# Between two transformer layers: paired powers, denominators on VectorE, and loads behind the first expert tiles

## The chip, the cores and the metric

The kernel runs on one core of a Trainium2 chip. The metric is the device time of one execution in microseconds (us). Matrix products run on TensorE (PE), elementwise work on VectorE (DVE), ScalarE (ACT) and GpSimd (POOL); SyncE (SP) issues most of the DMAs. The engines run side by side and wait for one another by semaphores only.

## The reference, cut to what matters

Thirty-two sequences of 128 rows of width 128 pass two layers, each with a residual attention and a residual feed-forward block. Layer 0's feed-forward block is a routed one with eight experts, and its routing is what the change touches:

```python
x = x + xattn0(layernorm(x), ctx, ctx)
n = layernorm(x)                          # eps 1e-5
num = einsum('bsd,ed->bse', n, waff)
aff = num / (norm(n) * norm(waff) + 1e-9) # the denominators
tcr = one_hot(argmax(softmax(aff)), 8)    # the chosen expert
ranks = argsort(argsort(-aff, axis=1), axis=1)
dispatch = tcr * (ranks < cap)            # cap from mean(aff)
x = x + sum_e(gelu((n*dispatch_e) @ W1_e + b1_e) @ W2_e + b2_e)
x = x + xattn1(layernorm(x), ctx, mask)   # 16 heads of 64, a null key and value
x = x + bitlinear_ffn(layernorm(x))       # ternary weights, 8-bit activations
```

## The kernel before, in words

The program is written by hand for each engine: an engine runs its instructions in the order in which its function issues them, and every dependency across engines, and most within one, is a `wait_ge` on a semaphore.

**Layer 0's attention and routing** (`attention_routing_block`) loops over the 32 sequences b. Beside the attention, each finished row block r is normalised and routed. VectorE takes mean and variance (`residual_stats`, into `stats2`); GpSimd adds epsilon and takes the power -0.5 (`route_norm`, L235); the normalised rows `xn2` are written by GpSimd, from r = 27 on by VectorE (`route_scale`, L743); TensorE transposes them (`route_transpose`) and multiplies with the router's weights (`affinity`, L367); VectorE copies the eight scores out (`num_copy`). The 32 blocks are routed in five groups (`GROUPS`), the last two of four blocks each. For a group, GpSimd works out the denominators in five instructions (`denominators`, L247); VectorE chooses an expert for each row in ten (`choose`: reciprocal, affinity and its maximum, a one-hot choice `tcrb`, and `seen`, the running count per expert); TensorE turns the choices into places in a sorted list (`places`, L369), in the last group behind a product `countp` that gives the counts of all rows; VectorE reads the places off (`locate`). Then GpSimd sends each block's 128 rows to their places in DRAM by an indirect DMA (`scatter`, L270). The rows of block r can go once their group is located and `xn2` is there. After the loop GpSimd does block 30's norm, scatter 24, block 31's norm, the last denominators, and scatters 25 to 31, in that order.

**Between the layers.** When the last variance is there (`l0["done"]`), SyncE issues 17 loads (`sync_weights`, L1426: layer 1's value weights, norm scales and biases, masks, null key and value, two context blocks and three feed-forward weights); the constants' loads all count on one semaphore `w_in`. TensorE fills its gaps with sums over the experts' output weights (`sums_part`, L1000), in eight parts of eight products; then come products for layer 1 (`Setup.tensor`, L1641, L1644, L1649), which wait for `w_in` (15 loads) and VectorE's list.

**The expert block** (`expert_block`) turns the counts into a list of at most 39 tiles (VectorE, L1137 to L1149; `tau` is the tile's place, `eid` its expert; ready as `from_dve` LIST). SyncE waits for the list and all scatters, then loads tiles of 128 rows, six slots ahead (`sync_part`, L947: six loads, the store of `Cc`, then one load for each slot that comes free). TensorE transposes tile i (L1019), multiplies it up (L1027) and down (L1039); the order on TensorE is up(i+1), transpose(i+2), down(i). GpSimd copies each tile's weights, ScalarE does the Gelu, VectorE adds the bias and, from tile to tile, also ranks rows and prepares layer 1: the null key's shift at tile 4, masks and context statistics at 8, weight magnitudes at 10.

**Layer 1** (`attention_ffn_block`) then gathers the rows back and loops over the 32 sequences.

Of the kernel before, what the change touches and what calls it, by code (L numbers as in the profile page):

```python
# [5 lines left out]
ALU = mybir.AluOpType  # L6
# [38 lines left out]
def routing_state(nc, space, ctx):  # L45


    B, E, G = 32, 8, 8

    def sb(name, shape, dt=F32):  # L50
        return space.enter_context(nc.sbuf_tensor("r_" + name, shape, dt))

    def sem(name):
        return ctx.enter_context(nc.semaphore("r_" + name))

    t = dict(
        waffT=sb("waffT", [P, E]), wsq=sb("wsq", [P, E]), wsum=sb("wsum", [P, E]), wn=sb("wn", [P, E]),
        ones=sb("ones_f", [P, P]), ones_b=sb("ones_b", [P, P], BF16), before_t=sb("before_t", [P, P], BF16),
        weight=sb("weight", [P, E]), region=sb("region", [P, E]),
        vpe=sb("vpe", [P, 2]), rs2=sb("rs2", [P, B]), spread=sb("spread", [P, G]), xnorm=sb("xnorm", [P, G]),  # L60
        xnT=sb("xnT", [P, 2, P]), num=sb("num", [P, B, E]), den=sb("den", [P, 2, G, E]), aff=sb("aff", [P, B, E]),
        mval=sb("mval", [P, B]), tmp=sb("tmp", [P, G, E]), score=sb("score", [P, G, E]), smax=sb("smax", [P, G]),
        tcr=sb("tcr", [P, B, E]), tcrb=sb("tcrb", [P, B, E], BF16), gsum=sb("gsum", [P, E]),
        seen=sb("seen", [P, 6, E], BF16),
        place=sb("place", [P, G, E]), posf=sb("posf", [P, B]), pos_s=sb("pos_s", [P, B], I32),
        zeros=sb("zeros", [P, 704]))
    s = {n: sem(n) for n in ("w_in", "set", "wsq", "wsum_done", "wsum", "wn", "rs2", "den", "xn2", "xnt", "xnT",
                             "num_done", "num", "choice", "place_done", "place", "z_out", "scat")}
    return t, s


def attention_routing_block(nc, ctx, space, consts, x, ctxT, w, wr, x_res, xn2, stats2, psum, dram):
# [19 lines left out]
    LATE = 28  # L92

# [48 lines left out]
    countp = xp[:, S + 16:S + 16 + E]  # L142
# [51 lines left out]
    def pool_part(g, after_setup, before_loop):  # L194
# [51 lines left out]

        def denominators(q):  # L247
            a, z = GROUPS[q]
            cols, n = slice(a, z), z - a
            spread, xnorm, den = rt["spread"][:, 0:n], rt["xnorm"][:, 0:n], rt["den"][:, q % 2, 0:n, :]  # L250
            den_seq, first = rsem["den"], 5 * q
            g.wait_ge(rsem["rs2"], 2 * z)
            nc.gpsimd.tensor_scalar(spread, stats2[:, cols, 1], float(D), None, ALU.mult).then_inc(den_seq, 1)
            g.wait_ge(den_seq, first + 1)
            nc.gpsimd.tensor_tensor(xnorm, spread, half[:, 0:n], ALU.pow).then_inc(den_seq, 1)
            g.wait_ge(den_seq, first + 2)
            nc.gpsimd.tensor_tensor(spread, xnorm, rt["rs2"][:, cols], ALU.mult).then_inc(den_seq, 1)
# [29 lines left out]
        for b in range(B):  # L287
# [4 lines left out]
            if b >= 2:  # L292
                route_norm(b - 2)
# [11 lines left out]
        route_norm(B - 2)  # L305
        scatter(scattered)
        scattered += 1
        route_norm(B - 1)
        denominators(NG - 1)
# [3 lines left out]
    def tensor_part(pe, expert_sums_part):  # L313
# [55 lines left out]
        def places(q):  # L369
# [12 lines left out]
            if q == NG - 1:  # L382
                pe.wait_ge(rsem["choice"], 10 * q + 10)
                nc.tensor.matmul(countp, rt["ones_b"][:], rt["seen"][:, q + 1, :], start=True, stop=True)
            nc.tensor.matmul(at_, rt["before_t"][:], rows[:, a:z, :].rearrange("p b e -> p (b e)"),
                             start=True, stop=False, skip_group_check=True)
            for j in range(n - 1):
# [3 lines left out]
                             start=False, stop=True, skip_group_check=True).then_inc(rsem["place_done"], 1)  # L391

# [208 lines left out]
    def vector_part(dve):  # L601
# [27 lines left out]

        def choose_reciprocal(q):  # L630
            a, z = GROUPS[q]
            n, seq = z - a, rsem["choice"]
            dve.wait_ge(rsem["den"], 5 * q + 5)
# [41 lines left out]
        def choose(q):  # L675
            choose_reciprocal(q)
# [60 lines left out]
        def residual_stats(b, s):  # L737
# [3 lines left out]
            nc.vector.bn_aggr(stats2[:, b, :], bn2[:, s, :]).then_inc(x1_stats, 1)  # L741

        def route_scale(r):  # L743
            dve.wait_ge(rsem["rs2"], 2 * r + 2)
            dve.wait_ge(rsem["xn2"], r)
            nc.vector.tensor_scalar(xn2[:, r, :], x_res[:, r, :], stats2[:, r, 0:1], rt["rs2"][:, r:r + 1],
# [14 lines left out]
        for b in range(B):  # L761
# [35 lines left out]
            elif b >= 1:  # L797
# [11 lines left out]
        route_scale(B - 1)  # L809
        num_copy(B - 1)  # L810
# [4 lines left out]
                done=(x1_stats, 3 * B), half_done=(x1_stats, 3 * (B // 2)), exp_done=(exp_ready, 4 * B), pv_free=(oev_ready, B), actp_free=(rsem["xnT"], B), countp=countp, route=route)  # L815


def make_consts(nc, ctx):
    def sb(name, shape, dt=F32):
# [4 lines left out]
             mask=sb("head_rows", [P, 16]), mask4=sb("group_rows", [P, 4]), minus_half=sb("minus_half", [P, 32]), half=sb("half", [P, 32]))  # L824

    def pool_part(g):
# [4 lines left out]
        nc.gpsimd.memset(c["half"][:], 0.5)  # L831
        nc.gpsimd.memset(c["mask"][:], 1.0).then_inc(ready, 1)
# [34 lines left out]
def expert_block(nc, ctx, space, consts, w, psum, dram, route, l0, pos_g):  # L867
# [79 lines left out]
    def sync_part(sp):  # L947
# [7 lines left out]
        for i in range(XT):  # L955
            load(i)
        sp.wait_ge(from_dve, CDS)
# [168 lines left out]
    def vector_part(dve, layer1_setup):  # L1126
# [9 lines left out]

        seq.then(nc.vector.tensor_scalar(ne[:], l0["countp"], float(P - 1), 1.0 / P, ALU.add, ALU.mult))  # L1137
# [142 lines left out]
def attention_ffn_block(nc, ctx, consts, w, wff, early, x_res, psum, before, gathered, out):  # L1280
# [68 lines left out]
    w_in, p_set, setup_done = sem("w_in"), sem("p_set"), sem("setup_done")  # L1349
    sa_done = sem("sa_done")  # L1350
# [27 lines left out]
    N_W = 15 * 16  # L1378
# [47 lines left out]
    def sync_weights(sp):  # L1426
        sp.dma_start(Wv[:], w["Wv"]).then_inc(w_in, 16)
        for t, n in ((s1, "ln1_s"), (b1, "ln1_b"), (sc_, "lnc_s"), (bc, "lnc_b")):
            sp.dma_start(t[:], w[n].rearrange("(d a) -> d a", a=1)).then_inc(w_in, 16)
        sp.dma_start(so_row[:], w["lno_s"].partition_broadcast(P)).then_inc(w_in, 16)  # L1430
        sp.dma_start(bo_row[:], w["lno_b"].partition_broadcast(P)).then_inc(w_in, 16)
        sp.dma_start(mask8[:], w["maskT"]).then_inc(w_in, 16)
        sp.dma_start(mrow8[:], w["mask"].partition_broadcast(P)).then_inc(w_in, 16)
        sp.dma_start(nk_row[:], w["nk"].partition_broadcast(P)).then_inc(w_in, 16)
        sp.dma_start(nv_row[:], w["nv"].partition_broadcast(P)).then_inc(w_in, 16)
        sp.dma_start(nv_col[:], w["nv2"]).then_inc(w_in, 16)
# [190 lines left out]
    class Setup:  # L1627
# [52 lines left out]
        def masks(self, dve, part):  # L1680
            bs = slice(8 * part, 8 * part + 8)
# [373 lines left out]
    def scalar_part(act):  # L2055
        act.wait_ge(w_in, N_W)
# [345 lines left out]
    return dict(sync_early=sync_early, sync_weights=sync_weights, sync=sync_part, pool_setup=pool_setup, gpsimd=pool_part, tensor=tensor_part,  # L2402
# [4 lines left out]
def two_layers(nc, d, out):  # L2407
# [5 lines left out]
    with ExitStack() as ctx:  # L2413
# [31 lines left out]
        def _(sp):  # L2445
# [5 lines left out]
            ex["sync"](sp)  # L2451
# [74 lines left out]
```

## Time and profile before

| | |
|---|---|
| median of 3 runs | 812.02 us (808.96 to 813.08) |
| the profiled execution's own time | 812.02 us |
| its span, first to last instruction | 810.3 us |
| TensorE busy in the span | 763.3 us, 94% |
| VectorE, GpSimd, ScalarE busy | 673.7, 477.8, 440.4 us |
| mean granted TensorE clock | 0.983 of 2.4 GHz |

Busy time is the union of an engine's instructions over the span, and overlapping engines don't add up. Layer 0 ends at some 206 us, the expert tiles run from 222 to 307 us, and layer 1 fills the rest. Which of the engines sets the time of a stretch is read from the chain of waits: it goes back from the last instruction of a window to whatever released it.

### The profile page before, as it was taken

Reading aid. Unit: us, or ns where it says so; the run is one execution under the profiler, and the core shown is the slowest. Engines: PE = TensorE matmul, PEld = TensorE weight load, DVE = VectorE, ACT = ScalarE, POOL = GpSimd, SP = SyncE. Lnnn points to the kernel's source line nnn. Section 1 sums busy time; section 2 is a strip of 40 time slices with the busy share of each in tenths; the row PEclk is TensorE's granted clock in tenths of the full one; section 3 lists DMA queues with packets and bytes.
Section 4 is the critical chain, followed back from the end, with each engine's and each line's share of the span. In section 5 each row is a group of like instructions: output and inputs, shape, how many; then the busy total and the mean of one; then the engine's idle time right before and its main releaser. Section 6 shows DMA issues by size and latency. Waiting matters only on the chain.

```text
span 810.3 us, 28859 instructions
## 1 busy us (share of the span) xinstructions
PE 763.3 (94%) x10843; PEld 642.5 (79%) x10873; DVE 673.7 (83%) x1775; ACT 440.4 (54%) x1078; POOL 477.8 (59%) x912
## 2 busy tenths in 40 slices
PE   8999999998799997999999999999999999999973
PEld 6777777776699996788888888878888888888861
DVE  6888889877757764689998999989989999999876
ACT  4666666656066663455564554555545655556542
POOL 7767678887857763345564655645645546554334
PEclk9999999999999998999999999999999999999996
DMA  8986220000422211121141141241231212212130
GB/s 240 372 350 253 110 87 15 17 21 28 141 70 67 60 46 34 38 64 46 42 78 54 46 87 45 53 80 46 62 71 45 81 52 62 70 45 77 39 44 14
DMA packets 68253, 65.81 MB, mean 81 GB/s; under 512 B 23714, under 2 KB 49042, under 8 KB 68114
## 3 DMA queue, kind: packets, MB, share of 16 engines
q1 hardware_dynamic: 53250, 39.71, 18.8%
q10 hardware_dynamic: 12816, 20.06, 6.7%
q0 software_dynamic: 2048, 4.20, 1.8%
q8 instruction: 86, 1.41, 0.7%
q14 instruction: 53, 0.43, 0.2%
HBM read 35.89 MB, written 24.37 MB: 74 GB/s over the span
## 4 chain that ended last, share of the span: by engine, by line
PE 37%; DVE 29%; DMA 18%; issue 6%; SPq 6%; POOL 2%; ACT 1%; DVEq 1%; another core or an unknown queue 0%; POOLq 0%; ACTq 0%
DMA a_r_all<-a_r_rows 10%; DMA a_r_rows<-a_rT 7%; SPq L1464 6%; DVE a_mxf L2222 5%; PE psum L1039 4%; PE psum L432 4%; PE psum L421 4%; PE psum L1027 4%; PE psum L414 3%; DVE a_rT L2238 3%; DVE f_h L2311 3%; DVE a_oT L2247 3%; DVE f_hm L2317 2%; DVE f_xt L2296 2%; PE psum L403 2%
## 5 line engine op out<-in xcount | busy, mean ns | idle before, releaser
L2079 ACT ACTIVATE a_pT<-psum 128x512 f32<-128x512 f32 x128 | 69.5, 595 | 50.9 <-PE psum L1888 35.0
L1571 POOL TENSOR_TENSOR f_hd<-f_hmc,a_wmean 128x1 f32<-128x1 f32 x32 | 6.7, 210 | 133.1 <-DVE f_hr L2322 131.9
L720 DVE TENSOR_REDUCE l_mx<-psum 128x4 bf16<-128x512 f32 x128 | 81.8, 680 | 3.5 <-PE psum L403 1.9
L2222 DVE TENSOR_REDUCE a_mxf<-psum 128x8 f32<-128x1024 f32 x64 | 77.5, 1210 | 4.6 <-PE psum L1857 4.6
L1800 PEld LDWEIGHTS psum<-a_cTm,a_Wk 128*128 128x128 f32 x512 | 64.1, 191 | 19.8 <-issue 19.8
L1788 PEld LDWEIGHTS psum<-a_xT,a_Wq 128*128 128x128 f32 x512 | 65.0, 193 | 15.4 <-issue 14.0
L552 ACT ACTIVATE l_pT<-psum 128x512 f32<-128x512 f32 x128 | 70.5, 597 | 8.1 <-PE psum L421 7.8
L1565 POOL TENSOR_SCALAR f_hq<-f_ht 128x512 bf16<-128x512 f32 x31 | 60.3, 1946 | 20.0 <-ACT f_ht L2122 19.9
L1867 PE MATMUL psum<-a_qT,a_kT 64*128 64x128 f32 x1024 | 71.9, 281 | 0.0
L1788 PE MATMUL psum<-a_xT,a_Wq 128*128 128x128 f32 x512 | 70.3, 281 | 0.6 <-ACT a_xT L2062 0.6
L1835 PE MATMUL psum<-a_Wv,a_cTm 128*128 128x512 f32 x128 | 70.1, 633 | 0.2
L1800 PE MATMUL psum<-a_cTm,a_Wk 128*128 128x128 f32 x512 | 70.2, 281 | 0.0
L2122 ACT ACTIVATE f_ht<-f_h,f_big_m,f_hr 128x512 f32<-128x512 f32 x32 | 26.0, 814 | 81.1 <-DVE f_hr L2322 79.0
L1867 PEld LDWEIGHTS psum<-a_qT,a_kT 64*128 64x128 f32 x1024 | 63.0, 190 | 0.0
L1901 PE MATMUL psum<-a_pT,a_v 128*32 128x128 f32 x2048 | 62.8, 274 | 0.1
L1815 PE MATMUL psum<-a_Wo,a_oT 128*128 128x128 f32 x512 | 62.6, 276 | 0.0
L1901 PEld LDWEIGHTS psum<-a_pT,a_v 128*32 128x32 f32 x2048 | 53.9, 110 | 8.4 <-DVE a_oT L2247 4.3
L1815 PEld LDWEIGHTS psum<-a_Wo,a_oT 128*128 128x128 f32 x512 | 59.7, 192 | 0.2 <-issue 0.2
L421 PEld LDWEIGHTS psum<-negI,l_mx 128*128 128x128 bf16 x512 | 35.3, 100 | 25.0 <-DVE l_mx L720 22.7
L2109 ACT COPY a_v<-psum 128x512 f32<-128x512 f32 x64 | 37.5, 585 | 23.1 <-PE psum L1835 23.1
L2247 DVE TENSOR_TENSOR a_oT<-psum,a_r_all 128x512 f32<-128x512 f32 x64 | 42.1, 679 | 9.5 <-issue 5.9
L1100 ACT ACTIVATE e_hT<-psum,e_w1t 128x128 f32<-128x128 f32 x156 | 44.5, 368 | 6.5 <-issue 5.8
(313 smaller groups left out, 2067.9 us busy)
## 6 DMA issues: line engine op xcount, KB each, us to landing
sorted_x<-r_zeros ACTq DMA_DIRECT2D x12, 1408.0 KB, 7.1
a_r_all<-a_r_rows SPq DMA_DIRECT2D x124, 128.0 KB
e_xt<-sorted_x SPq DMA_DIRECT2D x39, 64.0 KB, 1.8
sorted_y<-e_yt ACTq DMA_DIRECT2D x39, 64.0 KB, 1.6
e_w<-in_E_W1b SPq DMA_DIRECT2D x1, 2064.0 KB
a_cin<-in_ctx SPq DMA_DIRECT2D x32, 64.0 KB, 2.6
out<-f_x SPq DMA_DIRECT2D x32, 64.0 KB, 2.2
x_res<-in_x SPq DMA_DIRECT2D x1, 512.0 KB, 5.5
```

The source lines that it names most:

```text
L421: last = nc.tensor.matmul(tp[k][:, j * S:(j + 1) * S], mx[:, b % 2, h:h + 1].to_broadcast([P, P]), negI[:], start=False, stop=(j == Q4 - 1 ...
L552: nc.scalar.activation(pT[:, k, :], tp[k], ACT.Exp, scale=SCALE).then_inc(exp_ready, 1)
L720: nc.vector.tensor_reduce(mx[:, s, Q4 * k:Q4 * k + Q4], maxp[k % 2].rearrange("p (h t) -> p h t", h=Q4), AX_X, ALU.max).then_inc(mx_ready, 1)
L1788: last = nc.tensor.matmul(bank[:, i * S:(i + 1) * S], Wq[:, 4 * half + i, :], xT[:, b % 2, :], start=True, stop=True)
L1800: last = nc.tensor.matmul(bank[:, i * S:(i + 1) * S], Wk[:, 4 * half + i, :], cTm[:, b % 2, :], start=True, stop=True)
L1815: last = nc.tensor.matmul(pa[:, 0:D], oT[:, p, :], Wo[:, p, :], start=(p == 0), stop=(p == NP - 1))
L1835: nc.tensor.matmul(bank, cTm[:, b % 2, :], Wv[:, 512 * half:512 * half + 512], start=True, stop=True).then_inc(v_done, 1)
L1867: last = nc.tensor.matmul(tp[e][:, i * S:(i + 1) * S], kT[r, b % 2, p, :], qT[r, b % 2, p, :], start=(half == 0 and i == 0), stop=(half == ...
L1901: last = nc.tensor.matmul(op[half][32 * j:32 * j + 32, i * S:(i + 1) * S], v[:, b % 2, 8 * half + 4 * e + i, part], pT[:, 2 * half + e, i ...
L2079: nc.scalar.activation(pT[:, 2 * half + e, :], tp[e], ACT.Exp, scale=SCALE).then_inc(exp_ready, 1)
L2222: nc.vector.tensor_reduce(mxf[:, 8 * half:8 * half + 8].rearrange("p (e h) -> p e h", e=2), psum[:, 0:2, :].rearrange("p e (h t) -> p e h ...
L2247: nc.vector.tensor_tensor(oT[:, 4 * half:4 * half + 4, :].rearrange("p n q -> p (n q)"), op[half], r_all[:, half, :], ALU.mult).then_inc(o ...
```

## The change

Five edits, all around the end of layer 0. (1) For blocks 28 to 31 VectorE writes both bases, variance + 1e-5 and 128 x variance, into `spans`, and GpSimd takes both roots in one power on two columns (`paired_roots`) in the place of `route_norm`. (2) The last group's denominators move from GpSimd to VectorE: three instructions ahead of the reciprocal, and both go ahead of block 31's `num_copy`. (3) The count product goes behind the places in the last group, into another bank, and VectorE waits for it where it starts the list. (4) On TensorE `affinity(31)` goes ahead of the third part of the expert sums, and all but three parts go behind the last places. (5) Of `sync_weights` five loads stay; twelve go behind the first six tile loads (`sync_late`), with semaphores of their own that their readers wait for. The constant `pair` costs six one-column memsets at the start.

```diff
+    PAIRED = GROUPS[-1][0]
-    countp = xp[:, S + 16:S + 16 + E]
+    countp = yp[:, 3 * S:3 * S + E]
...
+        def paired_roots(r):
+            i = r - PAIRED
+            g.wait_ge(rsem["spans"], i + 1)
+            nc.gpsimd.tensor_tensor(rt["roots"][:, i, :], rt["spans"][:, i, :], consts["pair"][:, 0, :], ALU.pow).then_inc(rsem["roots"], 1)
...
-            if b >= 2:
+            if b - 2 >= PAIRED:
+                paired_roots(b - 2)
+            elif b >= 2:
                 route_norm(b - 2)
...
-        route_norm(B - 2)
+        paired_roots(B - 2)
         scatter(scattered)
         scattered += 1
-        route_norm(B - 1)
-        denominators(NG - 1)
+        paired_roots(B - 1)
         for r in range(scattered, B):
             scatter(r)
...
-            if q == NG - 1:
-                pe.wait_ge(rsem["choice"], 10 * q + 10)
-                nc.tensor.matmul(countp, rt["ones_b"][:], rt["seen"][:, q + 1, :], start=True, stop=True)
             nc.tensor.matmul(at_, rt["before_t"][:], ...
...
                              start=False, stop=True, skip_group_check=True).then_inc(rsem["place_done"], 1)
+            if q == NG - 1:
+                pe.wait_ge(rsem["choice"], 10 * q + 10)
+                nc.tensor.matmul(countp, rt["ones_b"][:], rt["seen"][:, q + 1, :], start=True, stop=True).then_inc(rsem["place_done"], 1)
...
         route_transpose(B - 1)
+        affinity(B - 1)
         expert_sums_part(2, 3)
-        affinity(B - 1)
-        expert_sums_part(3, 5)
         places(NG - 1)
-        expert_sums_part(5, E)
+        expert_sums_part(3, E)
...
+        def last_denominators():
+            n, seq, den = B - PAIRED, rsem["last_den"], rt["den"][:, (NG - 1) % 2, 0:B - PAIRED, :]
+            dve.wait_ge(rsem["roots"], n)
+            nc.vector.tensor_tensor(rt["last_spread"][:], rt["roots"][:, :, 0], rt["roots"][:, :, 1], ALU.mult).then_inc(seq, 1)
+            dve.wait_ge(seq, 1)
+            nc.vector.tensor_tensor(den, rt["last_spread"][:].unsqueeze(2).broadcast_to([P, n, E]),
+                                    rt["wn"][:].unsqueeze(1).broadcast_to([P, n, E]), ALU.mult).then_inc(seq, 1)
+            dve.wait_ge(seq, 2)
+            nc.vector.tensor_scalar(den, den, 1e-9, None, ALU.add).then_inc(seq, 1)
...
             nc.vector.bn_aggr(stats2[:, b, :], bn2[:, s, :]).then_inc(x1_stats, 1)
+            if b >= PAIRED:
+                dve.wait_ge(x1_stats, 3 * b + 3)
+                nc.vector.scalar_tensor_tensor(out=rt["spans"][:, b - PAIRED, :], in0=consts["pair"][:, 1, :], scalar=stats2[:, b, 1:2],
+                                               in1=consts["pair"][:, 2, :], op0=ALU.mult, op1=ALU.add).then_inc(rsem["spans"], 1)
...
         route_scale(B - 1)
+        last_denominators()
+        choose_reciprocal(NG - 1)
         num_copy(B - 1)
         choose(NG - 1)
         locate(NG - 1)
...
+        for i, (first, second) in enumerate(((-0.5, 0.5), (1.0, float(P)), (EPS_BLOCK, 0.0))):
+            nc.gpsimd.memset(c["pair"][:, i, 0:1], first)
+            nc.gpsimd.memset(c["pair"][:, i, 1:2], second)
...
         for i in range(XT):
             load(i)
+        after_first_tiles()
         sp.wait_ge(from_dve, CDS)
...
+        dve.wait_ge(rsem["place_done"], l0["groups"] + 1)
         seq.then(nc.vector.tensor_scalar(ne[:], l0["countp"], float(P - 1), 1.0 / P, ALU.add, ALU.mult))
...
-    N_W = 15 * 16
+    N_W, N_LATE = 8 * 16, 5 * 16
...
     def sync_weights(sp):
         sp.dma_start(Wv[:], w["Wv"]).then_inc(w_in, 16)
-        for t, n in ((s1, "ln1_s"), (b1, "ln1_b"), (sc_, "lnc_s"), (bc, "lnc_b")):
+        for t, n in ((sc_, "lnc_s"), (bc, "lnc_b")):
             sp.dma_start(t[:], w[n].rearrange("(d a) -> d a", a=1)).then_inc(w_in, 16)
...
+        sp.dma_start(nv_col[:], w["nv2"]).then_inc(w_in, 16)
         sp.dma_start(mask8[:], w["maskT"]).then_inc(w_in, 16)
...
+    def sync_late(sp):
+        sp.dma_start(nk_row[:], w["nk"].partition_broadcast(P)).then_inc(null_in, 16)
+        sp.dma_start(nv_row[:], w["nv"].partition_broadcast(P)).then_inc(null_in, 16)
         for b in range(2):
             sp.dma_start(cin[:, b, :], w["ctx"][b]).then_inc(cin_ld[b], 16)
+        sp.dma_start(mrow8[:], w["mask"].partition_broadcast(P)).then_inc(late_in, 16)
+        for t, n in ((s1, "ln1_s"), (b1, "ln1_b")):
+            sp.dma_start(t[:], w[n].rearrange("(d a) -> d a", a=1)).then_inc(late_in, 16)
+        sp.dma_start(so_row[:], w["lno_s"].partition_broadcast(P)).then_inc(late_in, 16)
+        sp.dma_start(bo_row[:], w["lno_b"].partition_broadcast(P)).then_inc(late_in, 16)
         sp.dma_start(wf[:, 0, :], wff["gateT"]).then_inc(f_in, 16)
...
         def null_shift(self, dve, which):
             if which == 0:
                 dve.wait_ge(lift_seq, 4)
+                dve.wait_ge(null_in, 2 * 16)
...
         def masks(self, dve, part):
+            if part == 0:
+                dve.wait_ge(late_in, N_LATE)
```

## Rows read from the trace of the kernel before

**Rows 1.** The page: the span.

```profile
span 810.3 us, 28859 instructions
```

**Rows 2.** Chain of waits, 185 to 232 us: start us, us, what.

```profile
208.76 0.20 DVE r_aff L642
...
216.47 2.33 DMA sorted_x<-xy,r_pos_s
...
219.85 1.74 DMA e_xt<-sorted_x
```

**Rows 3.** Timeline, 196 to 236 us: start, us, engine, operation, idle before.

```profile
204.89 0.25 POOL L238 TENSOR_SCALAR r_vpe<-stats 128x1 f32<-128x1 f32 x1
...
205.22 0.57 POOL L240 TENSOR_TENSOR r_rs<-r_vpe,minus_half 128x1 f32<-128x1 f32 x1
...
207.29 0.29 PE L367 MATMUL psum<-r_waffT,r_xnT 128*128 128x8 f32 x2
...
208.73 1.10 POOL L270 DMA_INDIRECT sorted_x<-xy,r_pos_s  x1 [0.39 <-issue]
...
209.88 0.19 DVE L663 TENSOR_TENSOR r_tcrb<-r_score,r_smax 128x32 bf16<-128x32 f32 x1
...
210.76 0.17 PE L384 MATMUL psum<-r_seen,r_ones_b 128*128 128x8 bf16 x1 [1.30 <-DVE r_seen L673]
...
210.91 2.92 PE L1000 MATMUL psum<-e_w,e_gb 128*128 128x128 f32 x24
...
211.78 0.17 DVE L710 CAST r_pos_s<-r_posf 128x4 int32<-128x4 f32 x1
...
214.86 2.05 PE L1641 MATMUL psum<-a_Wo,a_nv_col 128*128 128x128 f32 x16 [1.02 <-DMA a_nv_col<-in_A_nv]
...
215.68 0.17 DVE L1149 CAST e_tau<-e_tauf 1x39 int32<-1x39 f32 x1
```

**Rows 4.** Timeline, 219 to 262 us: the first expert tiles.

```profile
218.47 1.88 PE L1649 MATMUL psum<-a_Wk,a_lift_col 128*128 128x512 f32 x4
...
219.85 6.36 SPq L951 DMA_DIRECT2D e_xt<-sorted_x  x6
...
221.72 0.30 PE L1019 MATMUL psum<-ident,e_xt 128*128 128x128 f32 x1 [1.38 <-DMA e_xt<-sorted_x]
...
222.38 1.97 PE L1027 MATMUL psum<-e_xtT,e_w1t 128*128 128x128 f32 x8 [0.35 <-ACT e_xtT L1089]
...
226.50 1.06 PE L1039 MATMUL psum<-e_w2t,e_hT 128*128 128x128 f32 x8
...
227.45 34.43 SPq L951 DMA_DIRECT2D e_xt<-sorted_x  x20
...
234.20 0.27 PE L1019 MATMUL psum<-ident,e_xt 128*128 128x128 f32 x1
...
237.17 1.23 DVE L1674 SCALAR_TENSOR_TENSOR a_Wk<-a_nk_row,a_Wk 128x1024 f32<-128x1024 f32 x1
```

**Rows 5.** Windows: stretch, width, busy PE, PEld, DVE, ACT, POOL; PEclk, DMA share, GB/s.

```profile
222.00:224.00 2.00, 1.65 (x9) 1.62 (x9) 2.00 (x5) 0.27 (x1) 0.87 (x2) 0.63 0.21 63
224.00:226.00 2.00, 1.65 (x8) 1.25 (x8) 0.91 (x5) 1.31 (x5) 0.00 (x0) 0.51 0.27 70
```

**Rows 6.** Timeline, 196 to 236 us, SyncE: second and last of 17 loads.

```profile
204.69 0.43 SPq L1429 DMA_DIRECT2D a_s<-in_A_ln_s  x1
...
211.89 0.43 SPq L1441 DMA_DIRECT2D f_wf<-in_F_downT  x1
```

**Rows 7.** DMA issues, 200 to 240 us: KB each, median us to landing.

```profile
f_wf<-in_F_downT SPq DMA_DIRECT2D x1, 256.0 KB, 6.1
...
a_nv_col<-in_A_nv SPq DMA_DIRECT2D x1, 0.5 KB, 5.4
```

**Rows 8.** Lines by form, 218 to 312 us: the power on two columns.

```profile
L1700 POOL TENSOR_TENSOR a_rs<-a_rt,minus_half 128x2 f32<-128x2 f32 x1 | 0.7, 729 | 0.1
```

**Rows 9.** One line's instructions: the one-column memset.

```profile
L226 POOL MEMSET r_weight<- x8: 98/98/99, 13.6 to 14.0; 128x1 f32 x8
```

More of the change, by code:

```diff
@@ L64, in routing_state @@
         seen=sb("seen", [P, 6, E], BF16),
+        spans=sb("spans", [P, 4, 2]), roots=sb("roots", [P, 4, 2]), last_spread=sb("last_spread", [P, 4]),
         place=sb("place", [P, G, E]), posf=sb("posf", [P, B]), pos_s=sb("pos_s", [P, B], I32),
@@ L67, in routing_state @@
     s = {n: sem(n) for n in ("w_in", "set", "wsq", "wsum_done", "wsum", "wn", "rs2", "den", "xn2", "xnt", "xnT",
-                             "num_done", "num", "choice", "place_done", "place", "z_out", "scat")}
+                             "num_done", "num", "choice", "place_done", "place", "z_out", "scat", "spans", "roots", "last_den")}
     return t, s
@@ L632, in choose_reciprocal @@
             n, seq = z - a, rsem["choice"]
-            dve.wait_ge(rsem["den"], 5 * q + 5)
+            if q < NG - 1:
+                dve.wait_ge(rsem["den"], 5 * q + 5)
+            else:
+                dve.wait_ge(rsem["last_den"], 3)
             nc.vector.reciprocal(rt["tmp"][:, 0:n, :], rt["den"][:, q % 2, 0:n, :]).then_inc(seq, 1)
@@ L675, in choose @@
         def choose(q):
-            choose_reciprocal(q)
+            if q < NG - 1:
+                choose_reciprocal(q)
             choose_affinity(q)
@@ L741, in residual_stats @@
             nc.vector.bn_aggr(stats2[:, b, :], bn2[:, s, :]).then_inc(x1_stats, 1)
+            if b >= PAIRED:
+                dve.wait_ge(x1_stats, 3 * b + 3)
+                nc.vector.scalar_tensor_tensor(out=rt["spans"][:, b - PAIRED, :], in0=consts["pair"][:, 1, :], scalar=stats2[:, b, 1:2],
+                                               in1=consts["pair"][:, 2, :], op0=ALU.mult, op1=ALU.add).then_inc(rsem["spans"], 1)
         def route_scale(r):
-            dve.wait_ge(rsem["rs2"], 2 * r + 2)
+            if r < PAIRED:
+                dve.wait_ge(rsem["rs2"], 2 * r + 2)
+                scale = rt["rs2"][:, r:r + 1]
+            else:
+                dve.wait_ge(rsem["roots"], r - PAIRED + 1)
+                scale = rt["roots"][:, r - PAIRED, 0:1]
             dve.wait_ge(rsem["xn2"], r)
-            nc.vector.tensor_scalar(xn2[:, r, :], x_res[:, r, :], stats2[:, r, 0:1], rt["rs2"][:, r:r + 1],
+            nc.vector.tensor_scalar(xn2[:, r, :], x_res[:, r, :], stats2[:, r, 0:1], scale,
                                     ALU.subtract, ALU.mult).then_inc(rsem["xn2"], 1)
@@ L814, in attention_routing_block @@
     return dict(sync=sync_part, gpsimd=pool_part, tensor=tensor_part, scalar=scalar_part, vector=vector_part,
-                done=(x1_stats, 3 * B), half_done=(x1_stats, 3 * (B // 2)), exp_done=(exp_ready, 4 * B), pv_free=(oev_ready, B), actp_free=(rsem["xnT"], B), countp=countp, route=route)
+                done=(x1_stats, 3 * B), half_done=(x1_stats, 3 * (B // 2)), exp_done=(exp_ready, 4 * B), pv_free=(oev_ready, B), actp_free=(rsem["xnT"], B), countp=countp, groups=NG, route=route)
 def make_consts(nc, ctx):
@@ L823, in make_consts @@
     c = dict(ready=ready, ident=sb("ident", [P, P]), negI=sb("negI", [P, P], BF16), identb=sb("identb", [P, P], BF16),
-             mask=sb("head_rows", [P, 16]), mask4=sb("group_rows", [P, 4]), minus_half=sb("minus_half", [P, 32]), half=sb("half", [P, 32]))
+             mask=sb("head_rows", [P, 16]), mask4=sb("group_rows", [P, 4]), minus_half=sb("minus_half", [P, 32]), half=sb("half", [P, 32]),
+             pair=sb("pair", [P, 3, 2]))
     def pool_part(g):
@@ L945, in sync_weights, with sync_part @@
         sp.dma_start(tile_no[:], w["tile_no"]).then_inc(w_in, 16)
-    def sync_part(sp):
+    def sync_part(sp, after_first_tiles):
         def load(i):
@@ L1349, in attention_ffn_block @@
     w_in, p_set, setup_done = sem("w_in"), sem("p_set"), sem("setup_done")
+    null_in, late_in = sem("null_in"), sem("late_in")
     sa_done = sem("sa_done")
@@ L2055, in scalar_part @@
     def scalar_part(act):
-        act.wait_ge(w_in, N_W)
+        act.wait_ge(late_in, N_LATE)
         act.wait_ge(setup_done, 4)
@@ L2400, in vector_part @@
         finish(f + 2)
-    return dict(sync_early=sync_early, sync_weights=sync_weights, sync=sync_part, pool_setup=pool_setup, gpsimd=pool_part, tensor=tensor_part,
+    return dict(sync_early=sync_early, sync_weights=sync_weights, sync_late=sync_late, sync=sync_part, pool_setup=pool_setup, gpsimd=pool_part, tensor=tensor_part,
                 setup=Setup(),
@@ L2450, in _ @@
             af["sync_weights"](sp)
-            ex["sync"](sp)
+            ex["sync"](sp, lambda: af["sync_late"](sp))
             for q in ex["done"]:
```

6 lines of the change are left out of this document (removed).

## The prediction

> **What bounds the kernel now.** I read three views. The page gives the span, 810.3 us [rows 1]; the execution's own time, 812.02 us, lies 1.7 above it and equals the median of the three runs, so sums made on the trace need no scaling. The chain of waits was read only between 185 and 232 us [rows 2], since every edit but the memsets lies there or is read shortly after; the timeline of the same stretch [rows 3, 4] then shows what stands beside the chain. What one saves there is kept: layer 1 starts from the last expert tile, and its loop shifts as a whole.
>
> The reader is to see one chain. GpSimd adds epsilon (204.89), takes block 31's root (205.22 + 0.57 = 205.79) and works on the denominators until 208.4; scatter 25 follows at 208.73 and scatter 31, the seventh, at 216.47: six intervals, 1.29 us each. It lands 2.33 later (218.80), the first tile's load goes out at 219.85, lands at 221.59, and TensorE starts at 221.72 after 1.38 idle [rows 2 to 4]. VectorE's list (215.85) and TensorE's setup products (end 218.47 + 1.88 = 220.35) come earlier and are next in line [rows 3, 4].
>
> **The change part by part.** *Roots and denominators.* A power on two columns took 0.73 us [rows 8]. It replaces an addition and a power on one, 205.79 - 204.89 = 0.90. Blocks 29 and 30 save the like; part of it goes into the four small instructions that write `spans` on VectorE, which I put at 0.17 each by the smallest VectorE rows here [rows 3]. Both roots of block 31 are there at about 205.5, 0.3 earlier. The five denominators leave GpSimd, which can then issue scatter 25 at 205.9 and not 208.73. Scatters 25 to 27 have their places; 28 to 31 need group 4's, so VectorE decides the rest.
>
> *VectorE.* After block 31's scaling (ends 205.9) come three instructions of 0.19 with some 0.03 for each semaphore, 0.7, and the reciprocal, 0.36: 206.95. The scores must be copied by then. Their product (207.29) stood behind eight products of the expert sums; without those it runs near 206.6, and the copy ends near 207.2. So the affinities start at 207.2 instead of 208.76 [rows 2, 3], 1.55 earlier. The choice is complete at 208.5 (before 209.88 + 0.19). The place products then start at once; before, they stood behind the count product, which began at 210.76 because it waits for `seen` [rows 3]. VectorE writes `seen` meanwhile, until 209.1, and reads the places at 209.1 to 209.95, where the trace has 211.95 (211.78 + 0.17): 2.0 earlier. The count product (0.17) is over before VectorE asks for it, so its new wait costs nothing; if it were late, only the list waits, and that has over 1 us of slack against the scatters. The list comes at 213.85.
>
> *Scatters.* Scatter 28 starts 0.3 after the places (scatter 25 sat idle for 0.39 [rows 3]), at 210.25, and 31 three intervals later, at 214.1: 2.4 before 216.47. The first tile load goes out at 217.45 and lands at 219.2.
>
> *TensorE.* Five parts of the sums now stand behind the places. Twenty-four products took 2.92 us [rows 3], so forty take 4.8, from 209.35 to 214.1. The setup products start there: the 1.02 us wait for `nv_col`, the twelfth load, goes, as it is now the fourth of five. They took 220.35 - 214.86 = 5.5, so TensorE is free at 219.5. That, not the tile's landing, is late next: the first tile starts 2.2 earlier and without the idle 1.38.
>
> *The clock.* After the 1.38 us idle [rows 4] the granted clock fell: 0.63 and 0.51 in two windows of 2 us [rows 5], that is to the 1.2 GHz level. That lost 2 x 0.37 + 2 x 0.49 = 1.7 us of full speed; up(0) took 1.97 for eight products that take 1.06 at 2.4 GHz [rows 4]. With the gap gone I expect the high level. I keep back 0.4 of the 1.7, because down(0) would then wait for the first Gelu; the start gains 1.3, and down(0) stands 2.2 + 1.3 = 3.5 us earlier than 226.50. Were this all, the kernel would take 808.5.
>
> *Twelve loads behind the first six tiles.* SyncE issues one load in (211.89 - 204.69)/15 = 0.48 us [rows 6], so tile 6's load is pushed back by 12 x 0.48 = 5.8. Before, it went out 227.45 - 219.85 = 7.6 after the first and, at 1.74 to land, was there at 229.2; TensorE took it at 234.20 [rows 2, 4]: a cover of 5.0 us. Now it goes out at 217.45 + 7.6 + 5.8 = 230.85 and lands at 232.6, while TensorE, 3.5 early, asks at 230.7. Transpose 6 waits 1.9 us, down(4) and all behind it with it, and runs 1.5 earlier than before instead of 3.5. Tile 7 follows 1.1 later, TensorE wants it 1.9 later; the wait occurs once. The readers of the late loads are safe: the null key's shift, before at 237.17 [rows 4], needs the first two of the twelve, issued by 224.5, and even 5.4 to land leaves five us; masks and weight magnitudes come later still.
>
> What does such a wait do to the clock? An idle stretch of similar size led to 1.2 GHz just above. If the clock falls again, the costs lie between 0 (the low stretch lies within the wait) and the 1.7 of [rows 5]. I take 1.1, nearer to the upper end, since a part of the low stretch will lie in the wait itself.
>
> The Trainium skill, "TensorE: Matmul & The Clock Gate", section "HAM oscillation — how this bites in real kernels", says that a wait for a DMA between groups of matmuls makes the array throttle again, so that the group behind it starts at half rate. The trace agrees at the first tile; by the page alone the sum would take the full 1.7.
>
> *Memsets.* Six one-column memsets at the start cost at most 6 x 0.10 [rows 9] and at least nothing; eight of them with eight others between them started within 0.4 us, so I take 0.1.
>
> **The rivals.** *(a) The forecast:* tile 6 waits, the clock falls: 812.0 - 1.5 + 1.1 + 0.1 = 811.7. For it: 5.8 us are put into a cover of 5.0, while TensorE comes earlier. Against it: all hangs on half a microsecond here and there.
>
> *(b) The wait, but the clock holds:* 812.0 - 1.5 + 0.1 = 810.6. For it: TensorE idled 1.30 before the count product with no fall.
>
> *(c) No wait at tile 6*, because SyncE issues faster than 0.48 us or the sixth tile's load does not pay the same gaps: 808.5; 808.0 with a warmer start of layer 1.
>
> *(d) Slower: the queue, not the issue.* The late loads bring 1.6 MB, and the last of them took 6.1 us to land; half a kilobyte took 5.4 behind others [rows 7]. If tile 6 stands behind them in the DMA engines, it lands near 229.1 (six tile loads from 217.45 at 6.4, eleven late ones at 0.48) + 6.1 = 235.2, 1.0 later than TensorE took it before, with the clock's 1.7 on top and 0.1: 814.8. It decides from the point where tile 6 lands after 234.1. Against it: before, seven scatters moved at the same time, and now the queue is empty when the late loads begin. The Trainium skill's "DMA: Bandwidth & Descriptors", section "Queues, rings and completion order", has each DMA engine take the descriptors of one issuing engine in ring order, which speaks for this case.
>
> *(e) The front gains nothing* (VectorE's three instructions or the sums behind the places eat what GpSimd saves): then tile 6 is 0.8 late against unchanged demand: 812.9.
>
> **How the numbers follow.** Chances: (a) 0.40, (b) 0.20, (c) 0.22, (d) 0.13, (e) 0.05. The range from 808.0 to 815.0 takes in all five with some of the spread of the runs before (808.96 to 813.08). This kernel's measurement can tell about 0.5%, 4.1 us, from no change. Below 807.96 lies only case (c) with something on top, such as an earlier return of the clock at layer 1's start: 0.15. Above 816.08 lies (d) with a second fall of the clock: 0.08. The rest, 0.77, is the same.
>
> **What would show it.** Right: scatter 31 near 214.1, transpose 0 near 219.5 with no idle before it, PEclk 1.00 there, then an idle stretch of some 2 us on TensorE ahead of the transpose of tile 6, released by that tile's DMA, and a low clock behind it. Wrong: no such stretch, or tile 6 landing within 1.8 us of an issue before 229, or a list later than the scatters. The prediction falls as a whole if the end of the expert tiles moves by more than 3.5 us either way.

## The result and the profile after

The kernel after took 813.43 us (median of 15 runs, 811.74 to 816.39). In the same runs the kernel before took 808.96 (804.75 to 813.08), 3.06 less than the median that the prediction started from. The ratio is 1.0064, 95% interval 1.0042 to 1.0085: slower by 0.6%.

The page of the kernel after gives a span 2.9 us longer than before [rows 1]:

```profile
span 813.2 us, 28862 instructions
```

In the chain of waits (start us, us, what) the last scatter lands as fast as before [rows 2]; the load of tile 6 does not:

```profile
217.28 2.22 DMA sorted_x<-xy,r_pos_s
...
226.48 0.43 SPq L1473
...
232.01 0.44 SPq L1484
...
233.76 5.40 DMA e_xt<-sorted_x
```

L1473 to L1484 are the twelve late loads. The reader is to see 5.40 us to landing, where the first tile had needed 1.74 [rows 2]. The timeline (start, us, engine, line, operation, idle before it and what ended it) answers to [rows 3, 4]:

```profile
206.31 0.72 POOL L252 TENSOR_TENSOR r_roots<-r_spans,pair 128x2 f32<-128x2 f32 x1 [0.44 <-DVE r_spans L765]
...
207.08 2.05 PE L1037 MATMUL psum<-e_w,e_gb 128*128 128x128 f32 x8
...
207.22 1.03 POOL L277 DMA_INDIRECT sorted_x<-xy,r_pos_s  x1 [0.20 <-issue]
...
210.61 0.19 DVE L662 TENSOR_TENSOR r_aff<-r_num,r_tmp 128x32 f32<-128x32 f32 x1
...
221.46 1.88 PE L1692 MATMUL psum<-a_Wk,a_lift_col 128*128 128x512 f32 x4
223.17 0.27 PE L1056 MATMUL psum<-ident,e_xt 128*128 128x128 f32 x1
...
232.21 0.27 PE L1056 MATMUL psum<-ident,e_xt 128*128 128x128 f32 x1
...
239.21 0.48 PE L1056 MATMUL psum<-ident,e_xt 128*128 128x128 f32 x1 [4.72 <-DMA e_xt<-sorted_x]
...
239.48 1.92 PE L1076 MATMUL psum<-e_w2t,e_hT 128*128 128x128 f32 x8
...
242.89 0.42 PE L1056 MATMUL psum<-ident,e_xt 128*128 128x128 f32 x1
...
245.82 0.27 PE L1056 MATMUL psum<-ident,e_xt 128*128 128x128 f32 x1
```

The transposes of tiles 0, 5, 6, 7 and 8 start at 223.17, 232.21, 239.21, 242.89 and 245.82. Ahead of tile 6 TensorE stands still for 4.72 us. From tile 6 to tile 8 it then takes 6.6 us; the kernel before took 3.8 (234.20 [rows 4] to 238.04, shown below), so some 2.8 are too many. The windows (stretch, width, busy PE, PEld, DVE, ACT, POOL, granted clock, DMA share, GB/s) show why:

```profile
206.00:208.00 2.00, 2.00 (x11) 2.00 (x11) 0.91 (x5) 0.00 (x0) 1.50 (x2) 0.50 0.44 154
...
234.00:236.00 2.00, 0.49 (x5) 0.30 (x3) 0.36 (x2) 0.12 (x1) 1.00 (x2) 1.00 0.78 269
236.00:238.00 2.00, 0.00 (x0) 0.00 (x0) 0.00 (x0) 0.00 (x0) 0.00 (x0) 1.00 1.03 322
238.00:240.00 2.00, 0.79 (x4) 0.79 (x5) 0.00 (x0) 0.28 (x2) 0.00 (x0) 0.55 0.38 104
240.00:242.00 2.00, 2.00 (x11) 2.00 (x11) 0.46 (x2) 1.24 (x5) 0.44 (x1) 0.50 0.40 105
```

From 236 to 238 no engine computes and the DMA engines are full: the late loads' bytes are moving (the last of them, issued at 232.01, took 6.5 us to land). Behind the wait the clock is at its 1.2 GHz level (0.50), and eight products take 1.92 us where [rows 4] had 1.06. The Trainium skill ("TensorE: Matmul & The Clock Gate", section "HAM oscillation — how this bites in real kernels") says that a wait for a DMA between groups of matmuls throttles the array again, so that the next group starts at half rate; the trace agrees here, with 1.92 us against 1.06.

The first window shows something that was not expected: the clock was low at the end of layer 0 as well, from 204 to 214, and eight products of the expert sums took 2.05 us there.

### The profile page after: what moved, and what is told of

It reads as the page before. It is cut to its first block, busy times and chain, and to the rows that moved or that the text cites. A ratio compares the mean times of both kernels' runs of the same rounds, so it can differ in the third digit from the quotient of the medians.

```text
span 813.2 us, 28862 instructions
## 1 busy us (share of the span) xinstructions
PE 767.3 (94%) x10843; PEld 648.2 (80%) x10873; DVE 677.7 (83%) x1782; ACT 440.9 (54%) x1078; POOL 472.8 (58%) x909
## 4 chain that ended last, share of the span: by engine, by line
PE 36%; DVE 30%; DMA 18%; SPq 7%; issue 6%; ACT 2%; POOL 1%; DVEq 1%; another core or an unknown queue 0%; POOLq 0%; ACTq 0%
DMA a_r_all<-a_r_rows 10%; DMA a_r_rows<-a_rT 7%; SPq L1507 6%; DVE a_mxf L2268 4%; PE psum L440 4%; PE psum L429 4%; PE psum L1076 4%; PE psum L422 3%; DVE a_rT L2284 3%; DVE a_oT L2293 3%; DVE f_h L2357 3%; DVE f_hm L2363 2%; PE psum L1064 2%; DVE f_xt L2342 2%; PE psum L411 2%
## 5 line engine op out<-in xcount | busy, mean ns | idle before, releaser
L1834 PEld LDWEIGHTS psum<-a_xT,a_Wq 128*128 128x128 f32 x512 | 64.4, 192 | 15.3 <-issue 13.9
```

The costliest lines, as they stand in the source:

```text
L1834: last = nc.tensor.matmul(bank[:, i * S:(i + 1) * S], Wq[:, 4 * half + i, :], xT[:, b % 2, :], start=True, stop=True)
```

## The experiments

Two theories stood first. **Q**: the late loads delay tile 6, that is the whole loss, and the front (edits 1 to 4) is a gain. **F**: the front itself costs. Each kernel ran side by side with the kernel before, and each ratio is against those runs. "Start 31" is the start of the value products of layer 0's last iteration on TensorE (L440 in the kernel after); stages are compared from there, so that chance in layer 0 does not count.

**1. front_only** and **2. late_only** split the change. front_only has edits 1 to 4, with all 17 loads where they were:

```diff
             af["sync_weights"](sp)
-            ex["sync"](sp, lambda: af["sync_late"](sp))
+            af["sync_late"](sp)
+            ex["sync"](sp, lambda: None)
```

> Edits 1 to 4 as in the changed kernel, but the twelve loads are issued at once behind the first five, before the list, as in the kernel before. Theory Q (the twelve loads behind the first tiles stand in the DMA queues ahead of tile 6 and cost the whole loss, while the front is a gain): no idle stretch ahead of tile 6's transpose, 2 to 4 us below the kernel before, ratio 0.995 to 0.998. Rival F (the front itself costs: spans on VectorE in layer 0, the sums behind the places): as slow as the changed kernel, ratio 1.003 to 1.007, although tile 6 does not wait.

Measured: 1.0054 (1.0032 to 1.0075), slower. Its chain shows a wait that no theory had:

```profile
216.57 6.05 DMA sorted_x<-xy,r_pos_s
...
223.68 1.77 DMA e_xt<-sorted_x
```

The last scatter was issued at 216.57 and landed 6.05 us later, against 2.33 before [rows 2], while SyncE's loads were still moving (the DMA share from 218 to 220 was 0.88, in the kernel before 0.10). TensorE then idled 3.80 us ahead of the first tile, and its clock was 0.50 from 226 to 230. The trace of the kernel before has the same thing in small: of its last seven scatters the first, issued among the loads at 208.73, took 5.2 us to land, the next ones 5.1, 5.0, 4.3, 3.4 and 3.3, and only the last 2.33. In front_only the last scatter is issued 2.8 us behind the last load, in the kernel before 4.6. So Q was half wrong: without edit 5 the bytes of the loads stand in the scatters' way. The time lies where F put it, but for another reason. The Trainium skill ("DMA: Bandwidth & Descriptors", section "Queues, rings and completion order") says that each DMA engine takes turns between the queues it has work for; that loads of SyncE's queue slow scatters of GpSimd's agrees with it.

late_only is the kernel before with edit 5 alone (`sync_weights` cut in two as in the change, `sync_late` behind the sixth tile load).

> The kernel before with edit 5 alone: twelve loads behind the first six tile loads. Theory Q: tile 6 is awaited for 3 to 5 us, the clock falls behind that wait, and the kernel is 5 to 7 us slower than before, ratio 1.006 to 1.009, more than the changed kernel loses. Rival F: within 1 us of before.

Measured: 1.0076 (1.0047 to 1.0105), as Q said. That edit 5 alone makes the kernel slower is shown by this run. Chain and timeline have the same wait at tile 6, without any edit of the front:

```profile
234.53 3.39 DMA e_xt<-sorted_x
```

```profile
237.96 0.44 PE L1020 MATMUL psum<-ident,e_xt 128*128 128x128 f32 x1 [3.31 <-DMA e_xt<-sorted_x]
```

**3. small_late** and **4. big_late** ask whether SyncE's time for twelve issues or the bytes make the wait. Both are the kernel after; small_late issues the four large loads (1.28 MB) early, as shown, and leaves eight small ones late; big_late the other way round.

```diff
+    def sync_early_rest(sp):
+        sp.dma_start(mrow8[:], w["mask"].partition_broadcast(P)).then_inc(late_in, 16)
+        sp.dma_start(wf[:, 0, :], wff["gateT"]).then_inc(f_in, 16)
+        sp.dma_start(wf[:, 1, :], wff["upT"]).then_inc(f_in, 16)
+        sp.dma_start(wf[:, 2, :].rearrange("p (c d) -> p c d", c=FC), wff["downT"].rearrange("(c p) d -> p c d", p=P)).then_inc(f_in, 16)
...
             af["sync_weights"](sp)
+            af["sync_early_rest"](sp)
```

> The changed kernel, but the four large loads (the mask rows and three feed-forward weights, 1.28 MB) are issued early; the eight small ones (0.32 MB, 3.8 us of SyncE's issue time) stay behind the first six tiles. Theory Q: tile 6 lands within 2.5 us of its issue and TensorE waits under 1 us; ratio 0.996 to 1.000. Rival S (SyncE's issue time, not the bytes, delays tile 6): it goes out 3.8 us later than without late loads, TensorE waits 0.5 to 1.5 us, and most of the loss stays, ratio 1.002 to 1.005.

> The changed kernel, but the eight small loads are issued early and only the four large ones (1.28 MB, 1.9 us of issue time) stay behind the first six tiles. Theory Q: tile 6's load goes out 1.9 us later than without late loads but lands 4 to 6 us behind its issue; TensorE waits 2 to 4 us; ratio 1.001 to 1.005. Rival S: tile 6 lands 1.8 us behind its issue and TensorE does not wait; ratio 0.995 to 0.999.

Measured: 0.9987 (0.9962 to 1.0011) and 1.0014 (0.9991 to 1.0038). The transposes of tiles 5 and 6 in small_late, then in big_late:

```profile
229.91 0.27 PE L1056 MATMUL psum<-ident,e_xt 128*128 128x128 f32 x1
...
232.03 0.29 PE L1056 MATMUL psum<-ident,e_xt 128*128 128x128 f32 x1
```

```profile
228.96 0.27 PE L1056 MATMUL psum<-ident,e_xt 128*128 128x128 f32 x1
...
231.35 0.33 PE L1056 MATMUL psum<-ident,e_xt 128*128 128x128 f32 x1
```

They stand 2.12 and 2.39 us apart; in the kernel after it was 7.00. So neither is enough alone: big_late's bytes leave some 0.3 us of a wait, the small loads' issues none. But both come close. In big_late the bytes do delay the landing, as Q said, only the load goes out earlier:

```profile
227.19 4.12 DMA e_xt<-sorted_x
```

Counted from the first tile load, tile 6's load goes out 9.5 us later in big_late and lands 4.1 behind that, 13.7 in all. In small_late it is 11.4 and 1.9, 13.3 in all, in the kernel after 13.2 and 5.4, 18.6. TensorE wants the tile at 13.4 in the first two and at 13.9 in the kernel after. So the long wait needs both, the time of the twelve issues and their bytes. The wait expected for big_late, 2 to 4 us, was too high.

**5. spread, 6. spread_only, 7. spread_order.** If only the place of the loads costs, they should be harmless where there are few at a time. In spread each of the tile loads 6 to 11 is followed by two late loads (`sync_late`, by pairs). spread_only has this and nothing else of the change, spread_order this with edits 3 and 4:

```diff
-        after_first_tiles()
         sp.wait_ge(from_dve, CDS)
...
+            if i < 6:
+                behind_tile(i)
...
+    def sync_late(sp, pair):
+        if pair == 0:
+            sp.dma_start(nk_row[:], w["nk"].partition_broadcast(P)).then_inc(null_in, 16)
+            sp.dma_start(nv_row[:], w["nv"].partition_broadcast(P)).then_inc(null_in, 16)
...
```

> The kernel after with its twelve late loads in pairs, one pair behind each of the tile loads 6 to 11 (1.6 MB over six tiles). Theory P (place of the bytes: the front is a gain, and the loss is what the loads delay): last scatter lands 2.3 us behind its issue, first transpose of tile 6 some 2.1 us behind that of tile 5, ratio to before 0.994 to 0.998. Theory F (the front's edits cost by themselves, 0.27 us per late iteration and more): no wait at tile 6 either, and still 0.999 to 1.003. If a tile of 7 to 12 waits over 1 us for its load instead, the spread is not sparse enough and neither is told.

> The kernel before with the same spread of the twelve late loads and nothing else changed. Theory P: no wait at tile 6, and a front whose chain is not made of loads, so 0.998 to 1.001. If the loads beside the scatters cost something in the kernel before too, it gains: 0.995 to 0.997, as much as spread does, and then the front's edits are worth nothing.

> The spread of the loads with the order on TensorE alone (31's affinity ahead of the sums, count product behind the places); roots and denominators stay on GpSimd as before. If the paired powers and the denominators on VectorE are a gain (predicted: last scatter about 2 us earlier with them), this is 0.999 to 1.001 and above spread by 0.002. If the spans on VectorE cost what the denominators give back, it is equal to spread or below it.

Measured: 0.9984 (0.9957 to 1.0012), 0.9985 (0.9957 to 1.0012) and 0.9976 (0.9951 to 1.0001). No tile behind the first waited for its load (tiles 5 and 6 stand 2.12 apart in all three), and the slowdown was gone; this is shown. The landings themselves were still slow in places, up to 4.0 us in spread and 4.8 in spread_only, but no longer on a tile that TensorE was about to take. But the front's gain did not appear: spread has all of the front, spread_only none of it, and they are equal. The profile of spread tells where it went:

```profile
200.00:202.00 2.00, 0.99 (x7) 0.80 (x8) 1.72 (x11) 1.20 (x4) 1.67 (x3) 0.94 0.10 33
202.00:204.00 2.00, 1.61 (x11) 1.14 (x9) 1.60 (x10) 0.40 (x2) 0.30 (x1) 0.50 0.09 33
...
206.00:208.00 2.00, 2.00 (x12) 2.00 (x11) 0.88 (x6) 0.00 (x0) 1.60 (x2) 0.50 0.42 100
```

At the end of layer 0 the clock falls to 1.2 GHz behind a stretch in which TensorE was busy for half the time. What stands ahead of block 31's affinity (16 products of the sums, transposes, affinities) then takes twice as long (in big_late TensorE was as little busy from 200 to 202, 0.98, and the clock held). That gave theory **C**: the low clock at the end of layer 0 eats the front's gain; against it **N**: the clock there is chance, and the front has no gain to show.

**8. warm, 9. only_warm, 10. warm_pool.** Ten products of the identity, `idle_products`, fill TensorE's waits there; they go to a bank that is free, and nobody reads them. warm is spread with them, only_warm spread_only, and warm_pool is warm with the spans of blocks 28 to 30 on GpSimd.

```diff
+        idle_products(7, 2)
         affinity(B - 4)
...
+        idle_products(1, 2)
         affinity(B - 3)
         o_transpose(B - 1, 1)
+        idle_products(2, 2)
         output(B - 1, 1)
```

> The kernel spread with ten products of a 128x128 identity put on TensorE where it idles at the end of layer 0: 7 ahead of 28's affinity (a wait of 1.01 us), 1 ahead of 29's, 2 ahead of the last output projection. Their results are not used. Theory C (the clock that falls between 198 and 216 in the kernels with the new order is what eats the front's gain): clock 1.00 from 204 to 216, last affinity product 15.5 us and first tile transpose 20.7 us behind the start of 31's value products (as in big_late, the one profile with the new order in which the clock held; 24.5 in spread), ratio to before 0.994 to 0.997. Theory N (the clock there is chance, and the front gains nothing by itself): the ratio stays at 0.998 to 1.001. If the products only fill idle time and the clock falls all the same, the profile shows it, and the time is as in spread.

> The kernel spread_only (before, with the loads spread) with the same ten products in the same three places. Theory C: its order already held the clock in two of three profiles, so 0.3 to 0.7 us at most: 0.997 to 0.999, and warm is faster by 0.002 to 0.003. Theory N: equal to warm.

> The kernel warm with the spans of iterations 28 to 30 on GpSimd (two operations of a column each) in place of VectorE; 31's stays on VectorE. If the span of 0.22 us on VectorE is what makes the iterations from 29 to 31 take 5.77 in place of 5.50 us, they take 5.50 again and the first tile transpose is 0.5 us earlier than in warm: ratio 0.0007 below that of warm, which the times can not tell but the trace can. If it is the pair's power or the scale that waits for it, the iterations stay at 5.77.

Measured: warm 0.9991 (0.9966 to 1.0016), only_warm 1.0011 (0.9981 to 1.0041), warm_pool 1.0005 (0.9977 to 1.0034). By the times alone N stands: none differs from before. By the traces C stands in part: in warm the clock was 1.00 from 200 to 218, and the first tile came 20.98 us behind start 31, close to the 20.7 expected. In warm_pool it fell just before 209 all the same and the first tile came at 24.60. So ten products don't hold it every time.

warm_pool settles the question of the spans. The value products of the last three iterations in the kernel after, in order_hold below (no spans) and in warm_pool (spans of 28 to 30 on GpSimd):

```profile
188.13 1.08 PE L440 MATMUL psum<-l_pT,l_v 128*32 128x128 f32 x32
193.91 1.08 PE L440 MATMUL psum<-l_pT,l_v 128*32 128x128 f32 x32 [0.38 <-DVE x_res L756]
199.68 1.08 PE L440 MATMUL psum<-l_pT,l_v 128*32 128x128 f32 x32 [0.38 <-DVE x_res L756]
```

```profile
187.55 1.08 PE L439 MATMUL psum<-l_pT,l_v 128*32 128x128 f32 x32
193.07 1.08 PE L439 MATMUL psum<-l_pT,l_v 128*32 128x128 f32 x32 [0.40 <-DVE x_res L756]
198.57 1.08 PE L439 MATMUL psum<-l_pT,l_v 128*32 128x128 f32 x32 [0.39 <-DVE x_res L756]
```

```profile
187.42 1.08 PE L444 MATMUL psum<-l_pT,l_v 128*32 128x128 f32 x32
192.94 1.08 PE L444 MATMUL psum<-l_pT,l_v 128*32 128x128 f32 x32 [0.40 <-DVE x_res L763]
198.45 1.08 PE L444 MATMUL psum<-l_pT,l_v 128*32 128x128 f32 x32 [0.38 <-DVE x_res L763]
```

The distances are 5.78 and 5.77, then 5.52 and 5.50, then 5.52 and 5.51. One small instruction on VectorE, of 0.22 us, costs 0.26 us or a little more of layer 0 in each of two iterations. On GpSimd it does not, but block 31's scaling then waits longer for its root (TensorE idles 0.91 us ahead of 31's transpose, 0.26 in warm), so nothing is won.

**11. hold and 12. order_hold.** hold is warm with eight more idle products, 3 ahead of 31's affinity and 5 ahead of the last places. order_hold has the same eighteen and neither edit 1 nor edit 2.

```diff
         route_transpose(B - 1)
+        idle_products(3, 1)
         affinity(B - 1)
         expert_sums_part(2, 3)
+        idle_products(5, 1)
         places(NG - 1)
```

> The kernel warm (all five edits, loads spread, ten idle products) with eight more idle products in the tail: 3 ahead of 31's affinity, 5 ahead of the last places. Theory C: the clock stays 1.00 from 200 to 220, first tile transpose 20.7 to 21.2 us behind the start of 31's value products, ratio to before 0.995 to 0.998. Theory N: the start is early in the profile and the ratio still 0.999 to 1.001, since low stretches elsewhere decide the time.

> The kernel spread_order (order on TensorE alone, roots and denominators on GpSimd as before, loads spread) with the same 18 idle products. The front's gain by parts, at a held clock: in the new order with edits 1 and 2 the last scatter is issued 15.5 to 15.8 us behind the start of 31's value products, in the order of before 18.2. If the denominators on VectorE carry it (as predicted, 1.55 us of affinities waiting for them), this comes at 17 to 18.2; if the order on TensorE carries it, at 15.5 to 16.5.

Measured: hold 805.5 us, 0.9963 (0.9940 to 0.9985), the only kernel with edits 1 to 5 whose interval lies below 1; order_hold 807.25, 0.9973 (0.9951 to 0.9996). The two are not told apart by their times. Their timelines, hold first: affinities, last scatter, first transpose.

```profile
197.07 1.08 PE L440 MATMUL psum<-l_pT,l_v 128*32 128x128 f32 x32 [0.38 <-DVE x_res L761]
...
206.25 0.19 DVE L667 TENSOR_TENSOR r_aff<-r_num,r_tmp 128x32 f32<-128x32 f32 x1
...
213.11 0.96 POOL L277 DMA_INDIRECT sorted_x<-xy,r_pos_s  x1 [0.30 <-DVE e_tau L1193]
...
218.26 0.30 PE L1062 MATMUL psum<-ident,e_xt 128*128 128x128 f32 x1
```

```profile
209.03 0.19 DVE L663 TENSOR_TENSOR r_aff<-r_num,r_tmp 128x32 f32<-128x32 f32 x1
...
216.83 0.96 POOL L277 DMA_INDIRECT sorted_x<-xy,r_pos_s  x1 [0.30 <-issue]
...
221.93 0.30 PE L1044 MATMUL psum<-ident,e_xt 128*128 128x128 f32 x1 [1.01 <-DMA e_xt<-sorted_x]
```

Start 31 is at 197.07 in hold and 198.57 in order_hold. The last scatter comes 16.04 and 18.26 us behind it, the first tile 21.19 and 23.36. In these two traces, with the clock held, edits 1 and 2 bring the first tile 2.2 us forward, and the order on TensorE alone brings nothing (23.36 against 23.43 before). The last scatter of order_hold had been expected at 17 to 18.2 if edits 1 and 2 carry the gain. The spans' 0.5 us lie ahead of start 31, so that some 1.7 of the 2.2 are left.

The times don't show this gain. order_hold lies below 1 as well, without edits 1 and 2, and eighteen idle products in the order of before were not run (ten brought nothing that the times show, only_warm): that the products alone bring the time is an open rival. Over all runs they go with a higher clock: the mean granted clock was 0.979 in spread and 0.985 in hold, 0.981 in spread_order and 0.987 in order_hold, with the kernel before at 0.982 beside the first of each and at 0.984 beside the second.

The first tile's distance from start 31 in all fourteen profiles:

| | clock held from 200 to 218 | clock fell in that stretch |
|---|---|---|
| edits 1 and 2 in it | 20.73 big_late, 20.98 warm, 21.19 hold | 23.14 small_late, 23.49 after, 24.48 spread, 24.60 warm_pool, 25.63 front_only |
| neither | 23.43 before, 23.37 spread_only, 23.33 only_warm, 23.36 order_hold | 24.03 late_only, 25.11 spread_order |

(In front_only the late landing of the scatter is in it too.) In the three profiles with edits 1 and 2 and a held clock the first tile comes 2.1 to 2.7 us earlier than in the four without them. Where the clock fell it comes between 0.3 us earlier and 2.2 later than in the kernel before: the gain is gone.

## Why the prediction was wrong

Its likeliest case (a) gave 811.7, 0.3 less than its base, and it put no change at 0.77; the kernel is 4.47 us, 0.6%, slower. The mechanism is that of rival (d), which had 0.13 and a loss of 2.8. That the range, 808.0 to 815.0, holds the 813.43 is luck: it stood on a base 3.06 too high, and from 808.96 it would have run from 804.9 to 811.9.

These lines of the kernel before (start 31, tiles 5 and 8, layer 1's first key products) and the last line, the key products of the kernel after, belong to what follows:

```profile
198.29 1.08 PE L432 MATMUL psum<-l_pT,l_v 128*32 128x128 f32 x32 [0.38 <-DVE x_res L735]
...
232.08 0.27 PE L1019 MATMUL psum<-ident,e_xt 128*128 128x128 f32 x1
...
238.04 0.27 PE L1019 MATMUL psum<-ident,e_xt 128*128 128x128 f32 x1
...
306.85 3.74 PE L1800 MATMUL psum<-a_cTm,a_Wk 128*128 128x128 f32 x32
```

```profile
314.68 3.74 PE L1846 MATMUL psum<-a_cTm,a_Wk 128*128 128x128 f32 x32
```

From start 31 to the key products it took 108.56 us before and 115.00 after. The forecast was 108.56 - 1.5 + 1.1 = 108.2, so it took 6.8 more than forecast: 2.8 by the wait at tile 6, 1.7 by the clock behind it, 2.3 by a first tile that came no earlier.

- **The step that failed is the landing of tile 6.** The prediction let it land 1.75 us behind its issue. Its issue came as worked out, 13.2 us behind the first tile load (7.6 + 5.8 = 13.4). But it took 5.40 to land, so the wait was 4.72 in place of 1.9. late_only shows the same without the front (3.39 to land, 3.31 of a wait); small_late and big_late show that the wait needs the bytes and the issues together, and in spread, where both are spread out, it is gone. The reason given against (d), that the queue is empty when the late loads begin, was no reason: they fill it themselves, 1.6 MB issued in 6 us.
- **The clock behind the wait** cost 2.8 and not 1.1: the upper bound of 1.7 came from a shorter idle stretch, 1.38 [rows 4].
- **The front.** Scatter 25 was predicted at 7.6 behind start 31 and came at 7.54 (207.22 - 199.68). The rest was right for a held clock, as hold has it: affinities 1.29 earlier (1.55 predicted), last scatter 2.14 (2.4), first tile 2.24 (2.2). In the profiled execution of the kernel after, the clock was low from 204 to 214; the affinities came 0.5 later, the last scatter 0.6 earlier (217.28 - 199.68 = 17.60 against 18.18), and the first tile 23.49 behind start 31 against 23.43: nothing gained. The prediction asked what the clock does behind its new waits, but not whether it holds ahead of the affinities.
- **The spans** were put at 0.17 each, to be paid out of what the powers save. They took 0.22 each, and the two iterations ahead of start 31 became 0.5 us longer in all.
- **The start of the tiles** was right: no idle ahead of the first transpose, and from tile 0 to tile 5 it took 9.04 us against 10.36 (232.08 - 221.72), 1.3 gained as predicted.
- **Memsets**: no cost to be seen; the first value products start at 14.68 in the kernel after and 14.98 in that before.
- **The base.** 812.02 was the median of three runs and the profiled one; over fifteen runs the median was 808.96. Sums against 812.02 placed every case 3 us too high.

Two things stay open. Layer 1 starts its key products 7.8 us later in the profile after than before, yet the span is only 2.9 longer: from there to the end it took 503.5 us before and 498.5 after, and between 497.0 and 502.9 in the twelve other profiles, with no link to an edit; the mean granted clock of that stretch was 0.98 both before and after. And fourteen profiles don't show whether the new order makes the clock fall more often: without idle products it fell in five of six profiles with that order and in one of three without it. The mean granted clocks over all runs point the same way (0.979 to 0.982 in these six kernels, 0.982 to 0.984 in before), but the other low stretches are in them too, and late_only, without that order, has 0.980.

## What to carry to other kernels

A load that is moved out of one critical stretch takes its bytes along: ask what else of that queue is waited for in the microseconds behind its new place, and spread large loads thinly behind loads that have cover. Hold a predicted gain behind a sparse stretch of TensorE against the clock as well: here it was there only in the profiles in which the clock held. Take the base from the median of many runs; three were too few here.

## What was not expected of the hardware

- The landing of one DMA varies with what is queued ahead of it and beside it: a 64 KB load took 1.74 us with no late loads ahead and 5.40 behind twelve loads of the same queue; a scatter of GpSimd's queue took 2.22 to 2.33 where SyncE's loads were all but through, and with more of them beside it up to 5.2 in the kernel before and 6.05 in front_only.
- How much low clock an execution gets differs between executions of one program. Runs of the kernel before lay between 802.88 and 814.50 us with mean granted clocks from 0.975 to 0.991, and the slower ones had the lower clock (correlation -0.5 to -0.7 in each of four sets of runs).
- SyncE spent 1.83 us on one issue in late_only (`upT`, 0.43 in the kernel after); the cause stays open.
